# Behind the expert tiles: key-variance tiles, products of the fixed rows and combinations in another order

## The chip, the core and the metric

One core of a Trainium2 chip runs the whole kernel. Its engines are TensorE (PE, its weight loads PEld), VectorE (DVE), ScalarE (ACT), GpSimd (POOL) and SyncE (SP), each with its own instruction stream; they meet in semaphores alone. The metric is the device time of one execution in microseconds, as the median of several runs; less is better.

## The reference, cut to what matters

The program is two layers of gated cross-attention and mixture-of-experts over x of 16 x 56 rows of 256. The change lies at the end of the first layer's mixture of experts:

```python
logits = _gelu(x @ rw1) @ rw2
probs = jax.nn.softmax(logits, axis=-1)
wgt, idx = jax.lax.top_k(probs, TOP_K)            # TOP_K = 2
for e in range(E):
    Ye = _gelu(x @ w1[e] + b1[e]) @ w2[e] + b2[e]
    Ce = _gelu(b1[e]) @ w2[e] + b2[e]
    for k in range(TOP_K):
        mask = idx[..., k] == e
        active = jnp.any(mask).astype(x.dtype)
        term = jnp.where(mask[..., None], Ye, Ce)
        out = out + active * wgt[..., k:k + 1] * term
...
x = x + jnp.tanh(g_ffn[0]) * _L0_ffn_ref(_layernorm(x, axis=-1), ...)
```

The second thing that is computed there belongs to the second layer's cross-attention, whose keys of the context are normalised: `kx = _ln(kx.reshape(b, sc, g, d), kxln_w, kxln_b)` with kx from `cond @ w_kv_x`. The kernel computes the variance of each of these keys beforehand.

## The kernel before, in words

The first layer has two blocks, and a block ends in a barrier of all engines. In `context_and_router` PE makes the keys of the context, 16 batches of 12 tiles of 125 rows, and DVE takes their statistics; of the last batch only the first 4 tiles (KEPT) are done there. The other 8 (MOVED) are done at the end of `experts`, the block of the change.

`experts` runs 11 tiles of 256 token slots (TILES) through the expert that owns each, double-buffered, and SP stores each result to `ys` in DRAM. All operands are split into two fp32r parts, so that a product is three matmuls. Behind the last expert tile the engines do this:

- **POOL** (L864 to L874) waits until all of `ys` is stored, gathers the row that stands for no token (L867, into `fixed`) and then, for the 7 token groups of 128 rows and both chosen experts, 14 gathers from `ys` (L871), in four groups, `GROUPS = [(0, 1), (2, 3), (4, 5), (6,)]`, each with a semaphore `gathered[g]`.
- **PE** (`key_tile(t)`, L983 to L1000) makes a key-variance tile: 12 matmuls of 512 columns into the pair of PSUM banks t % 2 (banks 4 and 5, or 6 and 7); from t = 2 on it waits until DVE has read tile t - 2. `rest()` (L1002 to L1008) is the product of the coefficients and the fixed rows: 7 outputs of 256 columns in plain fp32, into banks 0 to 3, and it signals `rest_psum`. It needs the gathered row of L867 and, beside that, nothing of the key tiles. It runs between key tiles 3 and 4.
- **DVE** (`key_tile(t)`, L1057 to L1061) takes 8 `bn_stats` of such a tile and frees its banks. `combine(g)` (L1063 to L1076) weighs the two gathered rows of each token of group g, adds the product of `rest()` from PSUM, and adds the sum to x: L1067, L1071, L1075, each waiting for the one before it. The order is written out by hand: key tiles 0 to 3; the wait for `rest_psum`; then in turn `combine(0)`, key tile 4, `combine(1)`, key tile 5, `combine(2)`, key tile 6, `combine(3)`, key tile 7; then four operations that make variances of the statistics (L1085 to L1088).

ACT and SP have nothing to do in this stretch once the last expert tile is on its way. The barrier behind it starts `self_attention`, which stores x (L1218), loads its weights (L1222) and takes the statistics of x (L775) first of all.

Of the kernel before, what the change touches and what calls it, by code (L numbers as in the profile page):

```python
# [133 lines left out]
MOVED = NT - KEPT  # L134
GROUPS = [(0, 1), (2, 3), (4, 5), (6,)]
# [654 lines left out]
def experts(nc, io, keep, ps, f):  # L790
# [5 lines left out]
    with ExitStack() as ctx:  # L796
        m = Mem(nc, ctx, "s3")
        s, xs, b1, b1_raw = f.s, f.xs, f.b1, f.b1_raw
# [24 lines left out]
        def turns(eng, turn):  # L823

            def body(c):
                for r in range(2):
                    turn(2 * c + r, r, c)
            loop(eng, None, TILES // 2, body)
            turn(TILES - 1, 0, TILES // 2)
            turn(TILES, 1, TILES // 2)  # L830

        with nc.Block() as block:
# [99 lines left out]
            def _(pe):  # L932
# [50 lines left out]
                def key_tile(t):  # L983
                    if t == 0:
                        pe.wait_ge(wk_lo_ready, K2)
                        pe.wait_ge(parts_loaded, 32)
                        pe.wait_ge(s["x_lo_ready"], TILES)
                    if t == 1:
                        pe.wait_ge(s["y_ready"], TILES)
                    if t >= 2:  # L990
                        pe.wait_ge(kx_read, t - 1)
                    n = 0
                    for k in range(K2):
                        for a, ws in ((ct_hi, (wk_hi, wk_lo)), (ct_lo, (wk_hi,))):
                            for w in ws:
                                for hf in range(2):
                                    mm = pe.matmul(kx[t % 2][:, hf, :], a[:, k, TT * t:TT * t + TT], w[:, k, 512 * hf:512 * hf + 512],
                                                   start=(n == 0), stop=(n == 5))
                                n += 1
                    mm.then_inc(kx_ready, 1)  # L1000

                def rest():  # L1002
                    pe.wait_ge(null_gathered, 16)
                    pe.wait_ge(s["fixed_loaded"], 16)
                    pe.wait_ge(s["gelu_done"], J8 * TILES)
                    for t in range(NX):
                        mm = pe.matmul(rest_ps[:, t, :], f.coef_t[:, t * P:t * P + P], f.fixed[:, :], start=True, stop=True)
                    mm.then_inc(s["rest_psum"], 1)  # L1008
                turns(pe, turn)
                for t in range(MOVED):  # L1010
                    key_tile(t)
                    if t == 3:
                        rest()

            @block.vector
            def _(dve):
# [40 lines left out]
                def key_tile(t):  # L1057
                    dve.wait_ge(kx_ready, t + 1)
                    for g in range(G):
                        ins = dve.bn_stats(st[:, G * t + g, :], kx[t % 2][:, g // 4, DH * (g % 4):DH * (g % 4) + DH])  # L1060
                    ins.then_inc(kx_read, 1)  # L1061

                def combine(g):  # L1063
                    ts = GROUPS[g]
                    dve.wait_ge(gathered[g], 16 * 2 * len(ts))
                    for t in ts:
                        steps.done(dve.scalar_tensor_tensor(out=acc[:, t, :], in0=yg[0][:, t, :], scalar=f.top[:, t, 0:1], in1=rest_ps[:, t, :],  # L1067
                                                            op0=ALU.mult, op1=ALU.add))
                    steps.wait()
                    for t in ts:  # L1070
                        steps.done(dve.scalar_tensor_tensor(out=acc[:, t, :], in0=yg[1][:, t, :], scalar=f.top[:, t, 1:2], in1=acc[:, t, :],  # L1071
                                                            op0=ALU.mult, op1=ALU.add))
                    steps.wait()
                    at = slice(ts[0], ts[-1] + 1)
                    steps.done(dve.scalar_tensor_tensor(out=keep.x[:, at, :], in0=acc[:, at, :], scalar=keep.gates[:, 2:3], in1=keep.x[:, at, :],  # L1075
                                                        op0=ALU.mult, op1=ALU.add))  # L1076
                turns(dve, turn)
                for t in range(4):
                    key_tile(t)
                dve.wait_ge(s["rest_psum"], 1)  # L1080
                for g in range(len(GROUPS)):
                    combine(g)
                    key_tile(4 + g)
                dve.wait_ge(kx_read, MOVED)
                steps.done(dve.tensor_tensor(dif, st[:, :, 1], st[:, :, 4], ALU.subtract))  # L1085
                steps.link(dve.tensor_tensor(sq, st[:, :, 2], st[:, :, 5], ALU.add))
                steps.link(dve.tensor_tensor(dif, dif, dif, ALU.mult))
                dve.scalar_tensor_tensor(out=keep.krs[:, B - 1, KEPT * G:NT * G], in0=dif, scalar=DH / 4.0, in1=sq,  # L1088
                                         op0=ALU.mult, op1=ALU.add).then_inc(var_ready, 1)
                dve.wait_ge(var_ready, 1)  # L1090
                steps.wait()

# [1445 lines left out]
```

## Time and profile before

| | |
|---|---|
| median of 3 runs | 2467.07 us |
| lowest, highest | 2463.65, 2467.97 us |
| the profiled execution's own time | 2462.99 us |
| its span, first to last instruction | 2461.1 us |
| mean granted clock of PE | 0.964 of full speed |
| the stretch of the change in it | 731.95 us (first key tile on PE) to 772.2 us (barrier) |

The profile is of one execution. Times below are microseconds from the start of the span. Starts of matmuls are recorded, their ends are modelled. An idle time in front of an operation stands in brackets with what ended it; "remote" means that the profile has a wait and a semaphore update but no instruction of its own to which it can put it, and "issue" that no wait is seen.

### The profile page before, as it was taken

How to read it: one execution, taken by the hardware profiler on the slowest of the kernel's cores; microseconds unless marked ns; L12 is line 12 of the kernel's file. 1: busy time of each engine (PE TensorE's matmuls, PEld its weight loads, DVE VectorE, ACT ScalarE, POOL GpSimd, SP SyncE). 2: the span in 40 equal slices, each digit the busy share in tenths (PEclk: the TensorE clock that was granted, in tenths of full speed). 3: DMA queues.
4: the chain of work that ended last, by engine and by line, in shares of the span. 5: the costliest groups of instructions: out<-in, count | busy, mean ns of one | idle time of the engine just before them, and what ended most of it. 6: DMA issues, size and time to landing. Idle time of an engine off the chain costs nothing. (4 is left out here: it accounts for less than half of the span.)

```text
span 2461.1 us, 37753 instructions
## 1 busy us (share of the span) xinstructions
PE 2305.7 (94%) x12485; PEld 2019.9 (82%) x12485; DVE 2005.9 (82%) x3874; ACT 1066.8 (43%) x1826; POOL 944.7 (38%) x640
## 2 busy tenths in 40 slices
PE   7999999999995788867999999999999999998998
PEld 5777777879993566646999999999999999997898
DVE  8999988877766878865888988888889888887347
ACT  1000101018872666642555555555555555555233
POOL 5555200200003244441455555554555555556000
PEclk9999999999997888878999999999999999999999
DMA  9677543347643111124122222212222222114511
GB/s 386 257 281 301 218 151 122 145 150 251 225 156 123 57 61 46 44 71 162 50 91 79 84 79 87 74 51 86 90 77 86 79 86 73 52 63 148 204 53 53
DMA packets 171773, 304.51 MB, mean 124 GB/s; under 512 B 58769, under 2 KB 140770, under 8 KB 166562
## 3 DMA queue, kind: packets, MB, share of 16 engines
q1 hardware_dynamic: 165650, 283.18, 33.3%
q0 software_dynamic: 6032, 20.20, 2.2%
q8 instruction: 48, 0.79, 0.1%
q14 instruction: 43, 0.35, 0.0%
HBM read 214.35 MB, written 89.00 MB: 123 GB/s over the span
## 5 line engine op out<-in xcount | busy, mean ns | idle before, releaser
L1971 PE MATMUL ps<-s_qc,s_ct 128*125 128x448 f32 x2304 | 522.5, 376 | 1.3 <-issue 1.3
L1999 PE MATMUL ps<-s_p_hi,s_cn 125*128 125x448 f32 x1536 | 472.5, 369 | 2.8 <-DVE s_p_lo L2094 2.3
L1971 PEld LDWEIGHTS ps<-s_qc,s_ct 128*125 128x125 f32 x2304 | 420.2, 187 | 50.4 <-issue 12.9
L1852 POOL TENSOR_TENSOR keep_x<-keep_x,s_sx 125x896 f32<-125x896 f32 x128 | 288.9, 2257 | 233.3 <-DVE s_mxh L2115 113.8
L577 DVE BATCH_NORM_STATS2 s_st<-ps 125x6 f32<-125x128 f32 x1472 | 304.8, 281 | 46.2 <-PE ps L447 39.1
L1916 ACT ACTIVATE s_sx<-s_sx 125x896 f32<-125x896 f32 x192 | 182.2, 949 | 350.6 <-DVE s_sx L2088 350.6
L1999 PEld LDWEIGHTS ps<-s_p_hi,s_cn 125*128 125x128 f32 x1536 | 289.6, 189 | 29.0 <-DVE s_p_lo L2094 5.0
L2075 DVE TENSOR_TENSOR s_sx<-ps,keep_krs 125x896 f32<-125x896 f32 x192 | 208.8, 1088 | 122.0 <-PE ps L1971 118.3
L1999 PE MATMUL ps<-s_p_lo,s_cn 125*128 125x448 f32 x768 | 281.5, 367 | 0.0
L2094 DVE TENSOR_TENSOR s_p_lo<-s_sx,s_p_hi 125x896 fp32r<-125x896 f32 x192 | 258.8, 1348 | 2.7 <-ACT s_p_hi L1921 2.7
L2115 DVE TENSOR_TENSOR s_mxh<-s_mxh,s_sx 125x896 f32<-125x896 f32 x128 | 217.3, 1697 | 0.1
L2088 DVE TENSOR_TENSOR s_sx<-s_sx,ps 125x896 f32<-125x896 f32 x192 | 206.7, 1076 | 0.3 <-PE ps L1985 0.3
L1921 ACT ACTIVATE s_p_hi<-s_sx 125x896 fp32r<-125x896 f32 x192 | 183.3, 954 | 11.3 <-DVE s_p_lo L2094 4.1
L1849 POOL TENSOR_TENSOR keep_x<-s_sx 125x896 f32<-125x896 f32 x32 | 69.2, 2163 | 249.5 <-DVE s_mxh L2115 216.9
L1860 POOL TENSOR_TENSOR s_cn<-s_cn_raw,s_cn 125x1024 fp32r<-125x1024 f32 x48 | 143.7, 2995 | 44.8 <-ACT s_cn L1927 44.8
L1999 PEld LDWEIGHTS ps<-s_p_lo,s_cn 125*128 125x128 f32 x768 | 145.2, 189 | 11.5
L1418 PE MATMUL ps<-s_w_hi,s_xq 128*112 128x512 f32 x192 | 98.2, 512 | 52.2 <-DVE s_qn L1537 39.9
L447 PE MATMUL ps<-s_wk_hi,l_hi 128*125 128x512 f32 x384 | 122.4, 400 | 15.1 <-DVE l_lo L543 12.8
L447 PE MATMUL ps<-s_wk_hi,l_lo 128*125 128x512 f32 x384 | 121.2, 397 | 0.0
L447 PE MATMUL ps<-s_wk_lo,l_hi 128*125 128x512 f32 x384 | 121.0, 396 | 0.0
L447 PE MATMUL ps<-s_wk_hi,s_hi 128*125 128x512 f32 x352 | 112.2, 400 | 0.0
L447 PE MATMUL ps<-s_wk_hi,s_lo 128*125 128x512 f32 x352 | 110.5, 395 | 0.0
(393 smaller groups left out, 4823.7 us busy)
## 6 DMA issues: line engine op xcount, KB each, us to landing
l_ahead<-in_ctxt SPq DMA_DIRECT2D x16, 1500.0 KB, 8.0
s_ct<-ct_hi SPq DMA_DIRECT2D x48, 500.0 KB, 4.4
s_ct<-ct_lo SPq DMA_DIRECT2D x48, 500.0 KB, 5.1
s_cn_raw<-in_ctx SPq DMA_DIRECT2D x48, 500.0 KB
l_raw<-in_ctxt SPq DMA_DIRECT2D x15, 1500.0 KB, 10.4
l_raw<-in_w SPq DMA_DIRECT2D x16, 1024.0 KB, 5.1
ct_hi<-l_hi SPq DMA_DIRECT2D x8, 1500.0 KB, 12.6
ct_lo<-l_lo SPq DMA_DIRECT2D x8, 1500.0 KB, 16.1
```

What stands on the lines that cost most here:

```text
L447: mm = pe.matmul(kx[0:TT, t % NB, hf, :], a[:, k, TT * t:TT * t + TT], w[:, k, 512 * hf:512 * hf + 512], start=(n == 0), stop=(n == 5))
L577: ins = dve.bn_stats(st[:, G * t + g, :], kx[0:TT, t % NB, g // 4, DH * (g % 4):DH * (g % 4) + DH])
L1852: pool.tensor_tensor(a, a, p[:, PR * w.pt:PR * w.pt + PR, :], ALU.add).then_inc(s["acc_ready"], 1)
L1860: pool.tensor_tensor(cn_lo[:, at, :], cn_raw[c][:, :, :], cn_hi[:, at, :].bitcast(F32), ALU.subtract).then_inc(s["cn_lo_ready"], 1)
L1916: act.activation(p, p, ACT.Exp).then_inc(s["exp_ready"], 1)
L1921: act.activation(p_hi[w.pr][:, :, :], p, ACT.Copy).then_inc(s["hi_ready"], 1)
L1971: mm = pe.matmul(sc[st % 2][:, j, :], a[:, k, at:at + TT], x[w.h][:, k, :], start=(c == 0), stop=(c == 5))
L1999: mm = pe.matmul(pv[:, k, :], x[:, t, k * P:k * P + P], y[w.vr][:, j, :], start=(t == 0 and c == 0), stop=(t == NT - 1 and c == 2))
L2075: dve.tensor_tensor(by_group(sx[w.h][:, tiles, :]), by_group(sc[st % 2]), krs_b[:, tiles, HG * w.h:HG * w.h + HG].unsqueeze(3).to_broadcas ...
L2088: dve.tensor_tensor(p, p, mb.unsqueeze(1).to_broadcast([TT, PR, QH]), ALU.subtract).then_inc(s["sub_ready"], 1)
L2094: dve.tensor_tensor(p_lo[w.lr][:, :, :], p, p_hi[w.lr][:, :, :].bitcast(F32), ALU.subtract).then_inc(s["lo_ready"], 1)
L2115: dve.tensor_tensor(mxh[:, :, :], a, sx[w.h][:, tiles, :], ALU.max).then_inc(s["mxh_ready"], 1)
```

## The change

PE runs all eight key tiles and then `rest()`. DVE takes all eight key tiles, makes the variances, waits for `rest_psum` and then does the four combinations in a row. No operation is added or removed.

```diff
                 turns(pe, turn)
                 for t in range(MOVED):
                     key_tile(t)
-                    if t == 3:
-                        rest()
+                rest()
...
                 turns(dve, turn)
-                for t in range(4):
+                for t in range(MOVED):
                     key_tile(t)
-                dve.wait_ge(s["rest_psum"], 1)
-                for g in range(len(GROUPS)):
-                    combine(g)
-                    key_tile(4 + g)
                 dve.wait_ge(kx_read, MOVED)
                 steps.done(dve.tensor_tensor(dif, st[:, :, 1], st[:, :, 4], ALU.subtract))
                 steps.link(dve.tensor_tensor(sq, st[:, :, 2], st[:, :, 5], ALU.add))
                 steps.link(dve.tensor_tensor(dif, dif, dif, ALU.mult))
                 dve.scalar_tensor_tensor(out=keep.krs[:, B - 1, KEPT * G:NT * G], in0=dif, scalar=DH / 4.0, in1=sq,
                                          op0=ALU.mult, op1=ALU.add).then_inc(var_ready, 1)
+                dve.wait_ge(s["rest_psum"], 1)
+                for g in range(len(GROUPS)):
+                    combine(g)
                 dve.wait_ge(var_ready, 1)
                 steps.wait()
```

## Rows read from the trace of the kernel before

**Rows 1.** The page, part 1: busy time of each engine, share, instructions

```profile
PE 2305.7 (94%) x12485; PEld 2019.9 (82%) x12485; DVE 2005.9 (82%) x3874; ACT 1066.8 (43%) x1826; POOL 944.7 (38%) x640
```

**Rows 2.** Waits from 731 to 773: who for whom, total us, times, longest

```profile
PE ps L997 <- DVE l_xs L1060: 7.3, 1, 7.3
DVE l_xs L1060 <- remote: 5.2, 1, 5.2
DVE l_h L1067 <- remote: 5.1, 1, 5.1
```

**Rows 3.** Timeline of DVE: start, us, line, operation, out<-in, count, idle before

```profile
734.94 1.68 DVE L1060 BATCH_NORM_STATS2 l_xs<-ps 125x6 f32<-125x128 f32 x8 [2.10 <-PE ps L997]
...
743.33 1.68 DVE L1060 BATCH_NORM_STATS2 l_xs<-ps 125x6 f32<-125x128 f32 x8 [1.11 <-issue]
750.09 0.87 DVE L1067 SCALAR_TENSOR_TENSOR l_h<-l_ht,l_top,ps 128x256 f32<-128x256 f32 x2 [5.08 <-remote]
...
751.92 0.75 DVE L1075 SCALAR_TENSOR_TENSOR keep_x<-l_h,keep_gates,keep_x 128x512 f32<-128x512 f32 x1
757.89 1.69 DVE L1060 BATCH_NORM_STATS2 l_xs<-ps 125x6 f32<-125x128 f32 x8 [5.22 <-remote]
759.49 0.86 DVE L1067 SCALAR_TENSOR_TENSOR l_h<-l_ht,l_top,ps 128x256 f32<-128x256 f32 x2
...
761.97 1.68 DVE L1060 BATCH_NORM_STATS2 l_xs<-ps 125x6 f32<-125x128 f32 x8
...
767.63 0.46 DVE L1067 SCALAR_TENSOR_TENSOR l_h<-l_ht,l_top,ps 128x256 f32<-128x256 f32 x1
...
769.06 1.67 DVE L1060 BATCH_NORM_STATS2 l_xs<-ps 125x6 f32<-125x128 f32 x8
770.77 0.27 DVE L1085 TENSOR_TENSOR l_xs<-l_xs 125x64 f32<-125x64 f32 x1
...
771.51 0.23 DVE L1088 SCALAR_TENSOR_TENSOR keep_krs<-l_xs 125x64 f32<-125x64 f32 x1
```

**Rows 4.** Timeline of PE, first or last matmuls of tiles 0, 4, 5, 6, 7

```profile
731.95 0.62 PE L997 MATMUL ps<-s_w_hi 128*125 128x512 f32 x2
...
743.22 3.28 PE L1007 MATMUL ps<-l_fixed,l_coef_t 16*128 16x256 f32 x14
746.44 0.74 PE L997 MATMUL ps<-s_w_hi 128*125 128x512 f32 x2
...
751.68 0.63 PE L997 MATMUL ps<-s_w_hi,s_w_lo 128*125 128x512 f32 x2
759.63 1.22 PE L997 MATMUL ps<-s_w_hi 128*125 128x512 f32 x2 [7.33 <-DVE l_xs L1060]
...
764.91 0.77 PE L997 MATMUL ps<-s_w_hi 128*125 128x512 f32 x2
```

**Rows 5.** Timeline of POOL: the first and the last of the 15 gathers

```profile
736.72 0.92 POOL L867 DMA_INDIRECT l_fixed<-ys,l_null_u  x1 [240.27 <-DMA ys<-s_y]
...
754.35 0.95 POOL L871 DMA_INDIRECT l_wx<-ys,l_posu  x1 [0.30 <-issue]
```

**Rows 6.** Sequencers' waits for the gathers: duration ns, first and last start us

```profile
L1065 DVEq EVENT_SEMAPHORE  x1: 21/21/21, 744.5 to 744.5; - x1
...
L874 POOLq EVENT_SEMAPHORE  x2: 43/43/43, 754.6 to 757.1; - x2
```

**Rows 7.** Stretches: us, busy PE, PEld, DVE, ACT, POOL, PE clock, DMA, GB/s

```profile
757.80:765.00 7.20, 5.37 (x13) 4.17 (x14) 7.00 (x25) 0.00 (x0) 0.00 (x0) 0.50 0.00 0
```

**Rows 8.** Timelines of PE and DVE while POOL scatters rows, the block before

```profile
484.97 1.70 DVE L549 TENSOR_TENSOR l_lo<-l_raw,l_hi 128x1500 fp32r<-128x1500 f32 x1
...
485.32 0.62 PE L447 MATMUL ps<-s_wk_hi,s_lo 128*125 128x512 f32 x2
...
487.03 1.68 DVE L577 BATCH_NORM_STATS2 s_st<-ps 125x6 f32<-125x128 f32 x8 [0.35 <-PE ps L447]
```

**Rows 9.** Timeline behind the barrier: DVE's first operation of the next block

```profile
772.30 0.20 DVE L1495 RECIPROCAL s_rscale<-keep_cols 128x8 f32<-128x8 f32 x1 [0.56 <-PEq L832]
```

## The prediction

> **What bounds the kernel now.** I first read the busy shares on the page [rows 1]: PE is busy for 94% of the span and DVE for 82%. That says nothing of the stretch of the change, 40 us out of 2461. The second view is the list of waits of that stretch [rows 2]. The reader is to see three long ones: DVE waits twice for something "remote", 5.1 us before `combine(0)` and 5.2 us before its key tile 4, and PE waits 7.3 us for DVE to read that tile. The third view is DVE's timeline [rows 3], and the fourth PE's [rows 4]. They show which wait ends last. The stretch ends with DVE's last variance operation (771.51 + 0.23 = 771.74 us [rows 3]); the next block begins at 772.30 [rows 9]. PE ends its last tile at about 768, POOL is through with its waits by 757.1 [rows 6]. So the end is set by DVE's chain: key tiles 0 to 3 at PE's pace, (743.33 - 734.94) / 3 = 2.80 us each, of which DVE works 1.68; then two stalls; then from 757.89 on DVE without a gap.
>
> **The two stalls are signals from PE that come late.** `combine(0)` at 750.09 waits for `gathered[0]` and for `rest_psum`. The first wait was over at 744.5 [rows 6]. The matmuls of `rest()` start at 743.22 and PE goes on to tile 4 at 746.44 [rows 4], so their signal was due at about 746.5 and came some 3.6 us later. Key tile 4 on DVE at 757.89 waits only for PE's tile 4, whose first matmul starts at 746.44; tile 0 took from 731.95 to 734.94 [rows 3, 4], 2.99 us, to reach DVE, so tile 4 was due at 749.43 and came 8.5 us late, while the last matmuls of tile 5 start at 751.68 [rows 4]. The matmuls ran on time by their records and their signals did not. What else is there: POOL issues its 15 gathers from 736.72 to 755.3 [rows 5], one per (754.35 - 736.72) / 14 = 1.26 us, and is past its waits for them at 757.1. The other place with indirect transfers by POOL, the scatter of the block before, shows a small case: a tile whose last matmuls start at 485.32 and end by the model at 485.94 reached DVE, idle from 486.67, at 487.03 [rows 8], 1.1 us late. Tiles 1 to 3 of our stretch, early in the gathers, were on time.
>
> Of this the Trainium skill says, in "Perfetto Trace Analysis", section Summary: the profiler window per engine type, that TensorE's end is an estimate, and the page's table of its life has the signal pushed when PSUM acknowledges the writes. The rows agree that the signal can part from the record, here by 3.6 and 8.5 us.
>
> **The change part by part.** No operation is added or removed; two things move.
>
> *`rest()` behind key tile 7 on PE.* PE runs eight tiles with no product between them. Tile t waits for DVE's reading of tile t - 2; DVE needs 1.68 us of every 2.80, so the wait is covered unless a signal is late. Tile 7 reaches DVE at 734.94 + 7 x 2.80 = 754.54. `rest()` took 746.44 - 743.22 = 3.22 us and began 0.11 before DVE took tile 3 [rows 3, 4], so now it goes from 754.43 to 757.65. Its gathered row has long been there. It issues no DMA, and nothing stands behind it on PE before the barrier. Banks 0 to 3 are its own, banks 4 to 7 those of the key tiles: no new wait for PSUM.
>
> *The combinations behind the variances on DVE.* DVE takes tile 7 from 754.54 to 756.22, and the four variance operations take 771.74 - 770.77 = 0.97 us [rows 3], to 757.2: hidden under `rest()`. The new wait on DVE, for `rest_psum`, has the four combinations behind it, and for them waits the barrier. A group of two takes 761.97 - 759.49 = 2.48 us when something follows it, the last one 769.06 - 767.63 = 1.43 [rows 3]; 3 x 2.48 + 1.43 = 8.87. All gathers have landed by 757.1, so `gathered` holds up none. The chain ends at 757.7 + 8.9 = 766.6. Set against 771.74 this is 5.1 us less: the profiled execution's own 2462.99 would become 2457.9. What follows the barrier moves as one.
>
> *What that sum hides.* It takes away 3.6 + 5 us of stall and puts nothing in their place. Without any late signal the old order would be: `combine(0)` 746.55 to 749.03; tile 4 from 749.43, 1.60 us (759.49 - 757.89), to 751.03; then in turn 2.48, 1.60, 2.48, 1.60, 1.43, and 1.71 for tile 7 (770.77 - 769.06), to 762.33; variances to 763.3. Every wait in it holds: the gathers of groups 1 and 2 are there by 749.5 and 754.6 (their last is issued at 736.72 + 8 or 12 x 1.26, and the last one of all took 757.1 - 754.35 = 2.75 from its start), and PE's tiles 6 and 7 are ready at 755.1 and 758.1. So of the schedules alone the new one is the worse, by 766.6 - 763.3 = 3.3 us. The reason can be read off: before, the 8.9 us of combinations fill DVE's idle 1.1 us per tile and begin at 746.5; after, DVE idles through tiles 4 to 7 and through part of `rest()`, and the combinations start 11 us later, with nothing beside them.
>
> The cost of the late signals in the new order is what the trace can't show. Its bounds: below, nothing (tiles 1 to 3 had none); above, a signal held until 757.89, when the gathers are over, as for tile 4. I take the middle, as much as before, since the four signals of tiles 3 to 7 fall into the same part of the same gathers.
>
> **The forecast.** Late signals cost the two orders about alike, and what remains is the difference of the schedules, +3.3 us. The median of the runs is 2467.07, 4.1 us above the profiled execution; 2467.07 + 3.3 = **2470.4 us**. It holds as well if timed executions have no such stalls in either order. Chance 0.38.
>
> **Rival 1: the stall goes.** The late signals come from `rest()` standing amid the gathers, and tiles alone get through, as tiles 1 to 3 did. Then the sum above is right: 2467.07 - 5.1 = 2462.0. For it: no tile was late before the product was put in. Against it: the scatter made a tile late with no such product beside it [rows 8]. Chance 0.26.
>
> **Rival 2: only the product's own signal is late,** by 3.6 as before, because it is that matmul's nature. Then 766.6 + 3.6 = 770.2, 1.5 us less: 2465.6. For it: it was the first late one. Against it: after it two tiles were later still, and POOL is done by then. Chance 0.14.
>
> **Rival 3, slower: PE is caught by a held tile.** Tile 5 is due at 748.9 and its signal is held to 757.89. PE can do tile 6 but not tile 7, which waits until DVE has read tile 5 at 759.6. By then PE has idled since 754.5; in the old trace it idled from 752.3 and the stretch from 757.80 to 765.00 has a granted clock of 0.50 (1.2 of 2.4 GHz) [rows 7], in which tile 6 took 764.91 - 759.63 = 5.28 us [rows 4]. So tile 7 runs until 764.9, `rest()` until 768.1, and the combinations, which can no longer fill any of this, until 777.0: 5.3 us later than before, 2472.4. It decides from the point where the hold lasts past 756 or so; shorter ones only eat the lead. For it: the same gathers at the same times. Against it: with a hold of 3.6 us only, the lead covers it. Chance 0.20.
>
> The Trainium skill has a rule that speaks for this rival. "VectorE: DVE Perf Modes", section The TRN2 errata, warns that completion increments at a high rate from one engine can deadlock another, and that kernels with dense ones from several engines should space them. The trace shows delays and no deadlock; by that rule the tiles' signals would be caught in the gathers' sixteen-fold increments again, and the time would be that of rival 3.
>
> **Rival 4: nothing is changed** because waits are merged or the order of the engines is another than written: 2467. Chance 0.02.
>
> **How the numbers follow.** About 0.2% (4.9 us, so 2462.1 and 2472.0) is what a measurement of this kernel can tell from no change. Rival 1 lies on the lower bound, rival 3 just beyond the upper one; half of each counts. With some scatter of the forecast: faster 0.17, same 0.62, slower 0.21. The range takes in rivals 1 and 3 with 1.5 us to spare, 2460.5 to 2474.0, and leaves out some 0.15.
>
> **What the profile will show.** If I am right in the steps: no PE gap between tiles 0 to 7 other than a late signal's; the variances before `rest_psum`; four combinations in 8.9 us without a gap. The forecast and rival 3 want a wait of DVE for "remote" among tiles 4 to 7; rival 3 wants a gap and half clock on PE before tile 7; rival 1 wants neither, and DVE's end at 766.6; rival 2 wants a late start of `combine(0)`, at about 761. I am wrong in kind if a combination waits for a gather, or if the time moves in another block.

## The result and the profile after

The changed kernel takes 2471.94 us, the median of 10 runs (2468.75 to 2474.33), against 2465.80 us for the kernel before in as many runs (2461.91 to 2467.97): a ratio of 1.0025 with an interval of 1.0016 to 1.0035. It is slower by 6.1 us. The profiled execution took 2468.75 us with a span of 2466.8; that is 5.7 us more span than before, of which 0.4 us lies ahead of key tile 0 on DVE (735.38 against 734.94) and 5.1 us between that tile and the next block.

Line numbers move a little: `bn_stats` is now L1059, the combinations are L1066, L1070 and L1074, the variances L1080 to L1083. First DVE's timeline of the kernel after (start and duration in us, line and operation, out<-in, count, idle before it and what ended that):

```profile
735.38 1.68 DVE L1059 BATCH_NORM_STATS2 l_xs<-ps 125x6 f32<-125x128 f32 x8 [2.10 <-PE ps L997]
...
743.76 1.68 DVE L1059 BATCH_NORM_STATS2 l_xs<-ps 125x6 f32<-125x128 f32 x8 [1.11 <-PE ps L997]
747.97 1.68 DVE L1059 BATCH_NORM_STATS2 l_xs<-ps 125x6 f32<-125x128 f32 x8 [2.52 <-PE ps L997]
757.90 3.27 DVE L1059 BATCH_NORM_STATS2 l_xs<-ps 125x6 f32<-125x128 f32 x16 [8.25 <-remote]
764.81 1.68 DVE L1059 BATCH_NORM_STATS2 l_xs<-ps 125x6 f32<-125x128 f32 x8 [3.64 <-PE ps L997]
...
767.27 0.22 DVE L1083 SCALAR_TENSOR_TENSOR keep_krs<-l_xs 125x64 f32<-125x64 f32 x1
768.23 0.87 DVE L1066 SCALAR_TENSOR_TENSOR l_h<-l_ht,l_top,ps 128x256 f32<-128x256 f32 x2 [0.73 <-PE ps L1007]
...
776.73 0.48 DVE L1074 SCALAR_TENSOR_TENSOR keep_x<-l_h,keep_gates,keep_x 128x256 f32<-128x256 f32 x1
777.85 0.06 DVE L1492 MEMSET s_eps<- 128x1 f32 x1 [0.64 <-PEq L832]
```

Tiles 0 to 3 start 2.80 us apart. Tile 4 was due at 746.58 (735.38 + 4 x 2.80) and starts at 747.97, 1.4 late. Tile 5 was due at 749.38 and starts at 757.90, 8.5 late, after a wait of 8.25 us; it shares one row of 16 operations with tile 6, since PE had done both by then. The next block starts at 777.85, where it started at 772.30 [rows 9].

PE's timeline of the kernel after:

```profile
749.70 0.73 PE L997 MATMUL ps<-s_w_hi 128*125 128x512 f32 x2 [0.38 <-issue]
...
752.13 0.62 PE L997 MATMUL ps<-s_w_hi,s_w_lo 128*125 128x512 f32 x2
759.64 1.21 PE L997 MATMUL ps<-s_w_hi 128*125 128x512 f32 x2 [6.88 <-DVE l_xs L1059]
760.65 1.05 PE L997 MATMUL ps<-s_w_lo,s_w_hi 128*125 128x512 f32 x2
...
764.71 3.48 PE L1007 MATMUL ps<-l_fixed,l_coef_t 16*128 16x256 f32 x14
```

Its two stretches, 757 to 765 and 745 to 757 (length, busy us of PE, PEld, DVE, ACT and POOL, granted clock, DMA share, GB/s):

```profile
757.00:765.00 8.00, 5.36 (x13) 4.00 (x14) 3.46 (x17) 0.00 (x0) 0.00 (x0) 0.57 0.05 16
745.00:757.00 12.00, 7.37 (x31) 5.26 (x29) 2.13 (x11) 0.00 (x0) 8.84 (x10) 1.00 0.35 104
```

PE has done tile 6 by 752.8 and then stands still for 6.88 us: tile 7 needs the banks of tile 5, and DVE has not been told that tile 5 exists. When it goes on, the stretch has a granted clock of 0.57, for the most part the lower of the two levels (1.2 of 2.4 GHz); two matmuls take 1.05 us in place of 0.63, and tile 7 takes until 764.8, that is 5.1 us in place of 2.8. Only then comes `rest()`, and only then the combinations.

POOL's gathers are 1.26 us apart as before [rows 5]; in this execution they start 1.3 us later:

```profile
739.22 1.01 POOL L871 DMA_INDIRECT l_ht<-ys,l_posu  x1 [0.30 <-issue]
...
755.63 0.95 POOL L871 DMA_INDIRECT l_wx<-ys,l_posu  x1 [0.30 <-issue]
```

And the waits from 731 to 785 (who for whom, us in total, times, longest), which answer to [rows 2]:

```profile
DVE l_xs L1059 <- PE ps L997: 11.6, 6, 3.6
DVE l_xs L1059 <- remote: 8.3, 1, 8.3
...
PE ps L997 <- DVE l_xs L1059: 6.9, 1, 6.9
```

Before there were two waits for "remote", of 5.1 and 5.2 us, the first of them for `rest_psum`. Now there is one, of 8.3 us, and `rest()` is on time (DVE starts at 768.23, PE ends at 768.19).

### The profile page after: what moved, and what is told of

It reads as the page before. It is cut to its first block and busy times, and to the rows that moved or that the text cites. A ratio compares the mean times of both kernels' runs of the same rounds, so it can differ in the third digit from the quotient of the medians.

```text
span 2466.8 us, 37753 instructions
## 1 busy us (share of the span) xinstructions
PE 2306.8 (94%) x12485; PEld 2021.3 (82%) x12485; DVE 2005.1 (81%) x3874; ACT 1066.6 (43%) x1826; POOL 947.6 (38%) x640
## 3 DMA queue, kind: packets, MB, share of 16 engines
q1 hardware_dynamic: 165650, 283.18, 33.3%
q0 software_dynamic: 6032, 20.20, 2.2%
## 5 line engine op out<-in xcount | busy, mean ns | idle before, releaser
L1919 ACT ACTIVATE s_p_hi<-s_sx 125x896 fp32r<-125x896 f32 x192 | 183.3, 955 | 11.3 <-DVE s_p_lo L2092 4.1
```

The costliest lines, as they stand in the source:

```text
L1919: act.activation(p_hi[w.pr][:, :, :], p, ACT.Copy).then_inc(s["hi_ready"], 1)
```

## The experiments

**What had to be told apart.** The theory after the result is that POOL's 14 gathers keep PE's completion signals from DVE, in both orders; the new order is slower because its schedule is longer in itself and because a held tile stops PE. The rivals are that the late signals come from the place of `rest()` among the tiles; from the DMA traffic that lands (bytes, rows, completion increments); or from POOL being busy at all; and that the extra time is not the holds' but the schedule's alone.

One measure serves all kernels, from traces: the stretch from DVE's start of key tile 0 to the first operation of the next block. It is 772.30 - 734.94 = 37.4 us before [rows 3, 9] and 777.85 - 735.38 = 42.5 us after.

### Both orders without the gathers

The 14 gathers and the waits for them are taken out of both kernels; `fixed` is still gathered.

```diff
-                for g, ts in enumerate(GROUPS):
-                    for t in ts:
-                        for k in range(2):
-                            pool.indirect_dma_start(yg[k][:, t, :], None, io.ys, ...).then_inc(gathered[g], 16)
...
-                for g, ts in enumerate(GROUPS):
-                    pool.wait_ge(gathered[g], 16 * 2 * len(ts))
...
-                    dve.wait_ge(gathered[g], 16 * 2 * len(ts))
```

The old order:

> The old order without POOL's 14 gathers of L871 and without the waits for them; the combinations take what lies in the two buffers, so the values of the first layer's experts are wrong. The gather of L867 for the fixed rows stays. Theory A (indirect transfers by POOL make PE's signals late): no wait for 'remote' on DVE, rest_psum at about 746.5, DVE's last variance at about 763.3 instead of 771.7, the time 8 us less than before, ratio about 0.9966. Rival B (the signals are late for a reason on PE or in this place of the program, gathers are innocent): the two waits of 5 us stay, ratio 1.000 or at most 0.1% less.

The new order:

> The new order, with the same taken out (the combinations take what lies in the two buffers). Theory A: key tiles 0 to 7 at 2.80 us on PE without a gap and at full clock, rest() ends at about 758, combinations end at about 767 instead of 777.2; ratio to before about 0.998, and 3.3 us more than the old order without gathers. Rival B: DVE waits 8 us for a tile again, PE's last tile at half clock, ratio about 1.0025.

Against a before of 2464.09 the old order takes 2456.16 us (0.9971, 0.9961 to 0.9981) and the new one 2458.75 us (0.9979, 0.9970 to 0.9989). The two differ by 2.6 us. DVE's timeline of the old order without gathers:

```profile
745.13 1.68 DVE L1054 BATCH_NORM_STATS2 l_xs<-ps 125x6 f32<-125x128 f32 x8 [1.11 <-PE ps L991]
748.35 0.87 DVE L1060 SCALAR_TENSOR_TENSOR l_h<-l_ht,l_top,ps 128x256 f32<-128x256 f32 x2 [1.53 <-PE ps L1001]
...
751.36 1.68 DVE L1054 BATCH_NORM_STATS2 l_xs<-ps 125x6 f32<-125x128 f32 x8 [0.43 <-PE ps L991]
```

and of the new order without gathers:

```profile
756.88 1.68 DVE L1053 BATCH_NORM_STATS2 l_xs<-ps 125x6 f32<-125x128 f32 x8 [1.11 <-PE ps L991]
```

No wait for "remote" is left in either, though `rest()` stands amid the tiles in the first. The stretches are 29.0 us (765.74 - 736.75) and 33.1 us (770.38 - 737.32). In the second, the granted clock was 0.81 from 756.8 to 760.7, where `rest()` ran, and `rest()` took 3.95 us, 0.7 more than the 3.28 it takes at full clock; without that it would be 32.4, which the next runs show. So the schedules differ by 3.4 us in the traces and by 2.6 us in the medians. The gathers cost the old order 37.4 - 29.0 = 8.4 us in its trace, 7.9 by the medians and 7.1 by the ratio ((1 - 0.9971) x 2464). They cost the new order 42.5 - 32.4 = 10.1 us in its trace, and 11.3 by its two ratios ((1.0025 - 0.9979) x 2466), each of them against other runs of the kernel before.

### Plain loads in place of the gathers

Is it the traffic? In the new order, SP issues 14 plain loads of the same size and with the same completion increments:

```diff
+                for r in range(2):
+                    sp.wait_ge(y_stored[r], 16 * ((TILES + 1 - r) // 2))
+                for g, ts in enumerate(GROUPS):
+                    for t in ts:
+                        for k in range(2):
+                            sp.dma_start(yg[k][:, t, :], io.ys[P * (2 * t + k):P * (2 * t + k) + P, :]).then_inc(gathered[g], 16)
```

> The new order with POOL's 14 gathers replaced by 14 plain loads of 128 KB each from ys, issued by SP (the rows are those of the first slots, not the chosen ones). Same bytes, same buffers, same semaphores with 16 increments each. Theory A in the form 'it is POOL's indirect transfers': no late signal, combinations end at about 767. In the form 'it is the traffic or the increments of the DMAs': a tile's signal is late by several us again while the loads run, some 10 to 15 us from 738 on. Rival B: as the changed kernel, end at 777.

Measured: 2457.54 us, one execution; tiles at 734.78, 737.58 and so on to 754.33, all on time, combinations from 757.55; the stretch is 767.16 - 734.78 = 32.4 us. But SP has issued the last of them at 743.3, before tile 4, and with the gathers no tile before tile 4 was late either. This run alone therefore decides little. Then the same plain loads issued by POOL:

```diff
-                            pool.indirect_dma_start(yg[k][:, t, :], None, io.ys, bass.IndirectOffsetOnAxis(f.posu[:, k, t:t + 1], 0)).then_inc(gathered[g], 16)
+                            pool.dma_start(yg[k][:, t, :], io.ys[P * (2 * t + k):P * (2 * t + k) + P, :]).then_inc(gathered[g], 16)
```

> The new order with the 14 gathers replaced by plain loads of 128 KB from ys that POOL itself issues (the rows of the first slots, not the chosen ones). Separates what is special about the gathers: if it is that POOL writes the descriptors, a tile's signal is late here too (DVE waits some us for a tile, end near 777 if it is tile 5); if it is the indirect form with one descriptor per row alone, no late signal, combinations end about 30 us after DVE takes tile 0, as in the run with SP's loads (767 of 735).

Measured: 2459.74 us, one execution, again no late signal, 768.78 - 736.39 = 32.4 us. POOL issues these loads 0.53 us apart from 739.85 to 747.4, and tile 4 comes on time at 747.58. The seven gathers below fill nearly the same time, 739.26 to 747.8, and there the same tile is 1.8 us late. A longer burst of plain loads might still do it. The next run tries that: POOL's plain loads, two behind each key tile. The added edit:

```diff
                     for t in ts:
+                        if t > 0:
+                            pool.wait_ge(kx_ready, t + 1)
                         for k in range(2):
```

> The kernel of the run before this one (pair t of POOL's transfers waits until PE has made key tile t), with each of the 14 indirect gathers replaced by a plain load of 128 rows of 1 KB by POOL. The rows come in a fixed order, so the combinations add the wrong experts' rows: that part of the computation is changed. The 14 plain loads of the earlier run were all issued within 7 us; here two follow each key tile, so the burst is as long as the gathers' (about 18 us, POOL's last one near 755 to 758), with the same bytes, the same sixteen-fold completion increments and the same waits of POOL. Theory 'indirect': only an indirect transfer holds up PE's signals; all eight key tiles reach DVE 2.80 us apart, no wait of DVE over 1.2 us among them, from tile 0 to the next block 32.4 us, time 2457 to 2461. Rival 'length of the burst': any transfers that POOL issues over 18 us hold them up; one of the tiles 4 to 6 comes at least 1.5 us late, tile 0 to the next block 34 to 37 us as with the paced gathers (37.1), time 2461 to 2465.

POOL's and DVE's timelines of that kernel:

```profile
741.32 0.63 POOL L873 DMA_DIRECT2D l_ht<-ys  x1
...
755.44 0.54 POOL L873 DMA_DIRECT2D l_wx<-ys  x1
```

```profile
754.65 1.68 DVE L1061 BATCH_NORM_STATS2 l_xs<-ps 125x6 f32<-125x128 f32 x8 [1.10 <-PE ps L999]
757.44 1.68 DVE L1061 BATCH_NORM_STATS2 l_xs<-ps 125x6 f32<-125x128 f32 x8 [1.11 <-PE ps L999]
```

The loads now run from 741.3 to 756.0, nearly 15 us, with a pause of 1.7 us between the later pairs, and nothing is late: 770.28 - 737.89 = 32.4 us. POOL's DMA queue carries the same 6032 packets and 20.20 MB over the whole kernel with the gathers and with POOL's plain loads. (Its time, 2461.48, is one execution, as is the 2459.37 of the kernel before beside it; only its trace is read.) So the bytes and packets that land, the increments of semaphores and POOL as the issuer are not enough: of what was tried, only indirect transfers made a signal late. A burst of plain loads that lasts longer than 7.5 us without a pause was not tried.

### How many gathers, how large, and when

**Half as many.** Only the first of each token's two rows is gathered, so 7 gathers; the waits ask for half as much.

```diff
-                        for k in range(2):
+                        for k in range(1):
```

> The new order with 7 of the 14 gathers, those of the first chosen expert; the other buffer keeps what lies in it, so the values of the first layer's experts are wrong. They end at about 747 instead of 756. If a signal is held until POOL is through, tile 4 is late by about 1 us and tile 5, due at 749, is on time: no gap on PE, end at about 767. If the hold doesn't depend on the gathers that are still to come, tile 5 comes at about 758 again and the end is at 777.

Measured: 2460.80 us, one execution. DVE's timeline of the kernel with seven gathers:

```profile
744.81 1.68 DVE L1059 BATCH_NORM_STATS2 l_xs<-ps 125x6 f32<-125x128 f32 x8 [1.11 <-issue]
749.39 3.26 DVE L1059 BATCH_NORM_STATS2 l_xs<-ps 125x6 f32<-125x128 f32 x16 [2.91 <-remote]
754.22 1.68 DVE L1059 BATCH_NORM_STATS2 l_xs<-ps 125x6 f32<-125x128 f32 x8 [1.56 <-PE ps L997]
```

Tile 4, due at 747.62, is 1.8 late; tile 5, due at 750.42, is not late: it is there when DVE has done with tile 4. The last of the gathers starts at 746.87, so the hold ends 2.5 us after that. 769.84 - 736.42 = 33.4 us, 1.0 over the plain loads.

**Half as large.** 14 gathers of 64 rows in place of 128.

```diff
-                            pool.indirect_dma_start(yg[k][:, t, :], None, io.ys, bass.IndirectOffsetOnAxis(f.posu[:, k, t:t + 1], 0)).then_inc(gathered[g], 16)
+                            pool.indirect_dma_start(yg[k][0:64, t, :], None, io.ys, bass.IndirectOffsetOnAxis(f.posu[0:64, k, t:t + 1], 0)).then_inc(gathered[g], 16)
```

> The new order with 14 gathers of 64 rows instead of 128 (the other halves of the two buffers keep what lies in them). Same number of indirect transfers, half the rows and bytes. If the hold goes with the number of rows (one descriptor or more for each), it is shorter or begins later: tile 5 on DVE before 755, end before 772. If it goes with the number and pace of the indirect transfers, and POOL's 0.95 us for each stays, tile 5 comes at 758 and the end is at 777. If POOL is itself quicker with 64 rows, the window ends earlier and the hold with it.

Measured: 2474.67 us, one execution, which reached tile 0 at 739.74, 4.4 us later than the kernel after. DVE's timeline of that kernel:

```profile
753.05 1.68 DVE L1059 BATCH_NORM_STATS2 l_xs<-ps 125x6 f32<-125x128 f32 x8 [3.25 <-remote]
763.63 3.27 DVE L1059 BATCH_NORM_STATS2 l_xs<-ps 125x6 f32<-125x128 f32 x16 [8.89 <-remote]
770.77 1.68 DVE L1059 BATCH_NORM_STATS2 l_xs<-ps 125x6 f32<-125x128 f32 x8 [3.88 <-PE ps L997]
```

Tile 4 is 2.1 late, tile 5 9.9 late; 783.61 - 739.74 = 43.9 us. A gather of half the rows takes POOL 0.91 us in place of 0.95, and the signals are held as long or longer. Rows and bytes are not what matters. Whether it is the number of gathers in a row or the time that they take together, these runs can't tell, since the gathers are always about 1.25 us apart.

**All of them later.** POOL waits for PE's last key tile before the first of the 14.

```diff
+                pool.wait_ge(kx_ready, MOVED)
                 for g, ts in enumerate(GROUPS):
```

> The new order with POOL's 14 gathers only after PE has signalled key tile 7. Theory A: tiles 0 to 7 without a late signal, tile 7 on DVE at about 755; then the 14 gathers run from 755 to 773, the signal of rest() falls into them and may be late by some us, the combinations follow the gathers and end at about 777. Rival B: DVE waits about 8 us for tile 5 although no gather has been issued, PE's tile 7 at half clock, the gathers from 765 on, end at about 785.

Measured: 2466.03 us, one execution. The eight tiles come at 733.67 to 753.22, all on time, and the first three combinations wait for their gathers; DVE's timeline:

```profile
760.11 0.87 DVE L1067 SCALAR_TENSOR_TENSOR l_h<-l_ht,l_top,ps 128x256 f32<-128x256 f32 x2 [4.21 <-DMA l_wx<-ys,l_posu]
...
765.41 0.87 DVE L1067 SCALAR_TENSOR_TENSOR l_h<-l_ht,l_top,ps 128x256 f32<-128x256 f32 x2 [2.69 <-DMA l_wx<-ys,l_posu]
...
770.61 0.87 DVE L1067 SCALAR_TENSOR_TENSOR l_h<-l_ht,l_top,ps 128x256 f32<-128x256 f32 x2 [2.61 <-DMA l_wx<-ys,l_posu]
```

775.27 - 733.67 = 41.6 us: the holds are gone, and as much is paid as waits for data (9.5 us in three waits).

### Where `rest()` stands

DVE in the new order, PE in the old one:

```diff
                     key_tile(t)
-                rest()
+                    if t == 3:
+                        rest()
```

> One part of the change alone: DVE's new order with rest() between key tiles 3 and 4 on PE, as before. By the schedule alone the combinations could start at 759, tile 7 then being 3 us later: end 1 to 2 us later than with rest() behind. By theory A two tiles are held as in the old order: tile 4 and tile 5 at 758, PE at half clock from 759.6, both tile 6 and 7 to come, so tile 7 reaches DVE at 768, the variances end at 771 and the combinations at 780: 8 us more than before, 2472 to 2474.

Measured: 2473.19 us, one execution. PE makes `rest()` from 744.59 to 747.8, then tiles 4 and 5, and after them waits 7.81 us. DVE's timeline of that kernel:

```profile
744.69 1.68 DVE L1060 BATCH_NORM_STATS2 l_xs<-ps 125x6 f32<-125x128 f32 x8 [1.11 <-PE ps L997]
759.75 3.26 DVE L1060 BATCH_NORM_STATS2 l_xs<-ps 125x6 f32<-125x128 f32 x16 [13.37 <-remote]
```

Tiles 4 and 5 come together at 759.75, and two tiles are still to be made at that point. 782.09 - 736.31 = 45.8 us, 3.3 more than with `rest()` at the end. So its place amid the tiles is not what makes signals late (without gathers none was), but it puts one tile more behind the hold. Of the change's two moves, the one on DVE alone, which is this kernel, costs 45.8 - 37.4 = 8.4 us, and the one on PE gives 3.3 of them back, by one trace of each kernel.

### Spreading the gathers

If a burst of gathers does it, breaking the burst should help. In the new order, groups 0 and 1 (8 gathers) go at once, groups 2 and 3 wait until PE has made its last key tile:

```diff
                 for g, ts in enumerate(GROUPS):
+                    if g == 2:
+                        pool.wait_ge(kx_ready, MOVED)
                     for t in ts:
```

> The new order; POOL issues the 8 gathers of groups 0 and 1 at once and the 6 of groups 2 and 3 after PE's signal of key tile 7. Theory A: the first 8 are over at about 749, before a signal is held for long; tiles 0 to 7 at PE's pace within 1 us, tile 7 at 755, rest() at 758; the 6 gathers run from 755 to 762 and land by 765; combinations 758 to 767 with at most 1 us of waiting: ratio to before about 0.998 (2459 to 2460). If the signal of rest() is held by the last six, its 3 to 5 us come on top: ratio 1.000.

Measured: 2459.88 us (11 runs, 2457.89 to 2463.31) against 2464.58 before: 0.9980, interval 0.9971 to 0.9989. DVE's and POOL's timelines of the kernel with split gathers:

```profile
748.00 1.68 DVE L1061 BATCH_NORM_STATS2 l_xs<-ps 125x6 f32<-125x128 f32 x8 [2.53 <-PE ps L999]
750.95 1.68 DVE L1061 BATCH_NORM_STATS2 l_xs<-ps 125x6 f32<-125x128 f32 x8 [1.27 <-remote]
752.84 1.68 DVE L1061 BATCH_NORM_STATS2 l_xs<-ps 125x6 f32<-125x128 f32 x8 [0.20 <-PE ps L999]
755.79 1.68 DVE L1061 BATCH_NORM_STATS2 l_xs<-ps 125x6 f32<-125x128 f32 x8 [1.27 <-PE ps L999]
```

```profile
748.15 0.95 POOL L873 DMA_INDIRECT l_wx<-ys,l_posu  x1 [0.31 <-issue]
756.02 0.95 POOL L873 DMA_INDIRECT l_ht<-ys,l_posu  x1 [6.92 <-PE ps L999]
```

Tiles 4 and 5 are 1.4 and 1.5 late, tile 7 0.8, and no combination waits for the second burst. 768.73 - 735.41 = 33.3 us, 9.2 less than after and 4.0 less than before. This kernel beats the one before by its interval, and the one after by the traces.

The same in the old order, with the second burst behind PE's tile 5, since the combinations come earlier there:

```diff
+                    if g == 2:
+                        pool.wait_ge(kx_ready, 6)
```

> The old order with the gathers split: groups 0 and 1 at once, groups 2 and 3 after PE's signal of key tile 5. If late signals are what both orders pay, the old one gains from the split as well: rest_psum late by 2 us or less, tile 4 on DVE at about 751, no gap on PE at half clock, then combination 1, tile 5, and so on as the second gathers land, last variance at about 767 instead of 771.7: 4 to 5 us less than before, ratio 0.998. If the split helped only because the combinations stood behind all tiles, nothing is gained: ratio 1.000.

Measured: 2460.90 us (10 runs, 2457.61 to 2461.78 but for one of 2597.89) against 2463.17: 0.9987, interval 0.9977 to 0.9997. DVE's timeline:

```profile
748.26 0.87 DVE L1069 SCALAR_TENSOR_TENSOR l_h<-l_ht,l_top,ps 128x256 f32<-128x256 f32 x2 [2.33 <-PE ps L1009]
...
751.99 1.68 DVE L1062 BATCH_NORM_STATS2 l_xs<-ps 125x6 f32<-125x128 f32 x8 [1.16 <-PE ps L999]
...
761.82 0.87 DVE L1069 SCALAR_TENSOR_TENSOR l_h<-l_ht,l_top,ps 128x256 f32<-128x256 f32 x2 [4.08 <-DMA l_wx<-ys,l_posu]
```

The gain, 770.57 - 735.86 = 34.7 against 37.4, is less than I had hoped for: combination 2 now waits 4.1 us for the second burst, and tile 4 came 1.5 us late at the lower clock (see the last section). Here the old order's shorter schedule is of no use, and the new order's late combinations are what leaves room for a pause. The two intervals overlap, so that the new order with split gathers beats the old one with them is read from the traces (33.3 against 34.7 us), not from the medians.

Last, the gathers paced, each pair behind a key tile of PE, with the wait shown for the paced plain loads above:

> The new order; POOL issues the pair of gathers of row block t only when PE has signalled t + 1 key tiles, so that a held signal stops POOL. Theory A with a hold that ends some 1.3 to 2.6 us after POOL's last issue: a late signal ends the burst that holds it, so no tile is late by more than about 3 us, PE has no gap of 5 us and no half clock, end between 767 and 771: ratio 0.998 to 0.9995. If a hold, once there, lasts its 8 us whatever POOL does, the end is at 777 or later.

Measured: 2464.12 us (10 runs) against 2463.17: 1.0004, interval 0.9995 to 1.0014. The expectation missed: a ratio of at most 0.9995 was hoped for, with no tile more than 3 us late and no lower clock. DVE's and POOL's timelines:

```profile
748.95 1.69 DVE L1061 BATCH_NORM_STATS2 l_xs<-ps 125x6 f32<-125x128 f32 x8 [1.61 <-PE ps L999]
754.63 3.27 DVE L1061 BATCH_NORM_STATS2 l_xs<-ps 125x6 f32<-125x128 f32 x16 [3.99 <-PE ps L999]
761.00 1.68 DVE L1061 BATCH_NORM_STATS2 l_xs<-ps 125x6 f32<-125x128 f32 x8 [3.11 <-PE ps L999]
```

```profile
751.73 0.95 POOL L873 DMA_INDIRECT l_wx<-ys,l_posu  x1 [0.30 <-issue]
754.86 0.95 POOL L873 DMA_INDIRECT l_ht<-ys,l_posu  x1 [2.18 <-PE ps L999]
```

A pair of gathers takes 2.52 us and a tile 2.80, so the wait hardly paced anything: POOL's first gather started at 740.33, when tile 1 was already there (740.08), and ten gathers ran without a pause. Tile 5, due at 751.28, was held until 754.63, 2.9 us after the tenth gather began; and then POOL, which waits for the same signals of PE, went on too. PE had idled for 2.36 us, and the granted clock was 0.57 from 756.3 to 760.3, in which most of tile 7 ran. 774.37 - 737.28 = 37.1 us.

### When a held signal comes through

Set beside each other, the held tiles come through shortly after the last gather of a burst has started:

| kernel | gathers in the burst | last one starts | held tile starts | tile late by |
|---|---|---|---|---|
| before [rows 3, 5] | 14 | 754.35 | 757.89 | 8.3 |
| after | 14 | 755.63 | 757.90 | 8.5 |
| `rest()` early | 14 | 756.14 | 759.75 | 8.8 |
| half rows | 14 | 759.61 | 763.63 | 9.9 |
| paced | 10 | 751.73 | 754.63 | 3.4 |
| split | 8 | 748.15 | 750.95 | 1.5 |
| seven | 7 | 746.87 | 749.39 | 1.8 |

In the kernel before and in the one with `rest()` early, tile 4 has `rest()` ahead of it. There the last column counts from 0.67 us behind the start of the tile's last matmuls (748.89 and 750.25), the distance at which DVE took tile 0 (734.27 and 734.94 in the kernel before). The release follows the last gather's start by 2.3 to 4.0 us, at about the time when that gather's rows land (2.75 us behind its start in the kernel before). In every kernel tiles 0 to 3 came on time, while four or five of the gathers had begun. The first signal after them that DVE waits for is 0.5 to 3.6 us late (in the kernel with `rest()` early it is already the one held to the end), and with eight gathers or more the next is held until the end of the burst. The longest delay is 1.5 to 3.4 us with seven to ten gathers in a row, 8.3 to 9.9 with fourteen.

That is the rule of this place, not of every burst. The block before holds 14 indirect scatters by POOL in a row [rows 8], in the kernel after from 476.64 to 496.3, with some of them longer than the others. DVE and POOL there, in the kernel after:

```profile
485.68 2.38 POOL L363 DMA_INDIRECT xs<-l_h,l_posu  x1 [0.30 <-issue]
488.22 1.68 DVE L577 BATCH_NORM_STATS2 s_st<-ps 125x6 f32<-125x128 f32 x8 [1.01 <-remote]
495.36 0.97 POOL L363 DMA_INDIRECT xs<-l_h,l_posu  x1 [0.30 <-issue]
497.14 3.27 DVE L577 BATCH_NORM_STATS2 s_st<-ps 125x6 f32<-125x128 f32 x16 [1.29 <-remote]
```

The last matmuls of the two tiles start at 485.62 and 493.98, so that they are 1.9 and 2.5 us late by the 0.67 us above; the two between them are there when DVE comes to them. No signal was held through the burst. Whether that is due to the direction of the transfers, to the longer ones among them, or to something else was not tried.

## Why the prediction was right or wrong

The prediction gave 2470.4 us in a range of 2460.5 to 2474.0, with most of the chance on a change within 0.2%; slower by 0.25% was measured, just beyond that bound. The time, 2471.94, lies in the range, 1.5 us above the forecast; 1.3 us of this closeness is luck, since the median of 3 runs from which the forecast started lay that much above the median of 10. By difference, which does not depend on which runs of the kernel before are taken, it forecast +3.3 us and +6.1 was measured.

**The schedules' difference of 3.3 us: right.** The traces show 32.4 against 29.0 us without late signals, 3.4; the medians without gathers differ by 2.6. Its parts too: the old order without late signals was to end its variances 28.4 us after tile 0 started, and ended them 28.4 after (765.18 - 736.75). Tiles are 2.80 us apart. `rest()` takes 3.28 us at full clock and hides the variances. The four combinations were to take 8.9 us and took 9.0 (777.21 - 768.23), without a gap, and no gather held them up. What follows the barrier moved as one: from the next block's start to the end of the span are 1688.8 us before (2461.1 - 772.30) and nearly 1689.0 after (2466.8 - 777.85).

**"The late signals cost both alike": the step that failed.** The forecast took the cost in the old order, 8.4 us (771.74 - 763.3), as that of the new one. It was 10.1: 7.7 us by which tile 7 starts late (759.64 in place of 751.94, since with the paced plain loads it starts 19.55 us behind tile 0), 2.2 us by which it takes longer at the lower clock (5.1 in place of 2.9 until `rest()` starts), and 0.2 us that `rest()` takes longer (3.48 against 3.28). The sum of the traces is 3.4 + 1.7 = 5.1 us. The medians say 6.1 for the whole; the 1 us between them is within the interval of the ratio, which is some 2.3 us either way (half of 0.0019, times 2466), and nothing here settles it.

**Rival 3 was what happened.** It said that tile 5 would be held until 757.89 (it was 757.90), that PE would do tile 6 and stand still before tile 7, start that at 759.6 (759.64), run it at half clock until 764.9 (764.8), end `rest()` at 768.1 (768.19) and the combinations at 777.0 (777.21); its 2472.4 is within 0.5 us of the measured 2471.9. The path is the one it described, but the agreement to 0.1 us is luck: the gathers of this execution started 1.3 us later than in the profile of the kernel before, and the hold ended 2.3 us behind the start of the last one in place of 3.5. One of its readings was wrong: it had PE idle since 754.5, but by the prediction's own sum tile 6 is done at 734.94 + 6 x 2.80 = 751.7, and PE went idle at 752.8. I gave this rival 0.20, and against it I had put that the hold might be of 3.6 us only. The rows spoke against that: the release of tile 4 at 757.89 came with the end of the gathers and not a fixed time after the tile, and that point stood past the 756 from which, as the prediction said itself, this rival decides. The change doesn't move the gathers. What should have been priced is not how long a signal is held but when the hold ends, and what is still to be done from then on: in the old order tile 4 and the rest of DVE's work, with PE's tiles 6 and 7 beside it; in the new one tile 7, `rest()` and four combinations in a row.

**Rival 1, the stall goes,** fell: signals of tiles that have no product among them are held as well. **Rival 2,** only `rest()`'s signal is late, fell with it: it was on time once the gathers were over. The forecast's marks for "the profile will show" separated these: a wait for "remote" among tiles 4 to 7, and a gap and the lower clock on PE before tile 7, the mark of rival 3.

**The clock.** Before the change the lower clock (0.50) came after PE had idled since 752.3, and cost nothing, since DVE had combinations to do [rows 7]. After it, 0.57 came after PE had idled since 752.8, and tile 7 stood on the path. About the same idle time turned from harmless to 2.2 us.

**Completion increments at a high rate.** The prediction set beside rival 3 a rule of the Trainium skill ("VectorE: DVE Perf Modes", section The TRN2 errata: completion increments at a high rate from one engine can deadlock another, and kernels with dense ones from several engines should space them). The time came out as that reading of it said. But the runs do not bear out the reason: plain loads with the same sixteen-fold increments, 0.53 us apart and so more than twice as dense, made no signal late. No run deadlocked, and what was seen is a delay that goes with the indirect gathers.

## What to carry to other kernels

Where a signal is held until some burst of work is over, ask what still has to run from that moment on: an order that leaves independent work for the waiting engine is worth more than one whose schedule looks tidier, and any tile that needs the held one's buffer stops the producer as well, and its clock falls. A burst of indirect gathers beside TensorE work was such a burst here. Breaking it (into 8 and 6, the second part behind the last key tile) was worth 0.2%, where reordering the work around it lost 0.25%. And two orders are to be compared with the disturbance taken away first: the schedules' difference, 3.4 us, could be read off beforehand, and the rest is what the disturbance does to each.

## What the runs showed of the hardware that I had not expected

- PE's completion signals reach DVE up to 9.9 us late while POOL runs indirect gathers one after another (0.95 us each, 1.26 us apart; 9.9 is with half rows, 8.5 in the kernel after). The matmuls themselves run on as if nothing were: in the kernel after, tile 6 ran from 749.70 to 752.75 while tile 5 was held. POOL's own wait on the same signals saw them as late (paced gathers).
- DVE's signals to PE are not held with them. In the kernel after, DVE ends its reading of tile 4 at 747.97 + 1.68 = 749.65, and tile 6 on PE, which waits for that, starts at 749.70, amid the gathers and while PE's signal of tile 5 is held.
- Plain loads of the same bytes by SP (0.47 us apart) or POOL (0.53 us apart, or in pairs over 15 us) hold nothing, and gathers of half the rows hold as much as whole ones. By what means the chip delays them stays open. The records show when the waiting engine goes on, not where a signal is in the meantime. The signals of ACT and SP were not looked at.
- The granted clock can fall where PE has not idled: in the old order with split gathers it was 1.00 from 735 to 747.3 with PE busy throughout, and 0.54 from 747.3 to 751. Tile 4 took 4.4 us there in place of 2.9 and arrived 1.5 us later for it; the same tile had a clock of 1.00 in the kernel before. In the new order without gathers it was 1.00 from 734.3 to 756.7 with PE busy throughout, and 0.81 from 756.8 to 760.7, where `rest()` ran. In both, `rest()` stands at or just ahead of the fall, but in the kernel before and with the plain loads it ran without one. No run here says what made the difference.
